# Decoder layer on one core: x rows in a home of their own, and the first attention's lead-in in a new order

## The reference

```python
u  = layernorm(x)
xn = layernorm(u) * gamma + beta
h  = dA * h + dB * xn[t]                       # a scan over the 1024 steps, 64 states per channel
y  = C . h + D * xn[t]
x1 = x + u + (y @ Wout.T + bout)
q  = layernorm(x1)                             # 16 heads of 16; keys and values are the context
x2 = x1 + softmax(q k.T / 4) v @ Wx.T + bx
z  = layernorm(x2)
g  = silu(z @ w1.T * s1) * (z @ w2.T * s2)     # 256 -> 1024, ternary weights with a scale per row
g  = gelu(g @ h1.T * t1);  g = gelu(g @ h2.T * t2)   # 1024 -> 1024, twice
out = x2 + g @ w3.T * s3
```

## Time and profile before

| what | us |
|---|---|
| median of 3 runs | 1010.57 |
| lowest, highest | 1008.23, 1010.67 |
| the profiled execution's own time | 1008.29 |
| its span, first to last instruction | 1006.6 |
| PE, DVE, ACT, POOL busy | 887.8, 527.2, 502.6, 188.1 |

### The profile page before, as it was taken

One profiled execution on the slowest core, in us unless ns is written; L12 is line 12 of the kernel. 1 busy time (PEld: TensorE's weight loads), 2 busy tenths in 40 slices (PEclk: granted clock), 3 DMA queues, 4 the chain that ended last, 5 costly groups with the idle time before them and its releaser, 6 DMA issues.

```text
span 1006.6 us, 15130 instructions
## 1 busy us (share of the span) xinstructions
PE 887.8 (88%) x5570; PEld 702.4 (70%) x5570; DVE 527.2 (52%) x877; ACT 502.6 (50%) x776; POOL 188.1 (19%) x207
## 2 busy tenths in 40 slices
PE   2038679669999999999999999999999999999996
PEld 0038567457787778777877777778777877777884
DVE  7975326455555555455545554556454645463411
ACT  2863514136644664466356635663566356635431
POOL 0864631022002200220022002200220021003000
PEclk9569889779999999999999999999999999999998
DMA  9976672510002000100010001000100020001000
GB/s 285 250 252 198 242 286 85 209 68 1 1 22 68 0 0 21 68 0 0 21 68 0 0 21 68 0 0 21 68 0 0 21 68 0 0 21 42 1 1 23
DMA packets 14632, 62.82 MB, mean 62 GB/s; under 512 B 2739, under 2 KB 4406, under 8 KB 13782
## 3 DMA queue, kind: packets, MB, share of 16 engines
q1 hardware_dynamic: 13862, 60.19, 17.5%
q10 hardware_dynamic: 704, 2.16, 0.7%
q0 software_dynamic: 32, 0.00, 0.0%
HBM read 50.16 MB, written 23.72 MB: 73 GB/s over the span
## 4 chain that ended last, share of the span: by engine, by line
PE 72%; DVE 12%; issue 7%; ACT 4%; DMA 4%; POOL 0%; SPq 0%; DVEq 0%; ACTq 0%; POOLq 0%
PE pair L1070 45%; PE pair L1057 10%; PE pair L1018 3%; DMA vblk<-in_ctx 3%; PE pair L1029 3%; PE pair L1045 2%; PE pair L462 2%; PE pair L995 2%; PE pair L1038 1%; DVE h1lo L889 1%; PE pair L469 1%; DVE tok L395 1%; DVE tok L391 1%; PE pair L527 1%; PE pair L476 1%
## 5 line engine op out<-in xcount | busy, mean ns | idle before, releaser
L1070 PE MATMUL pair<-h1hi,h_turned 128*128 128x512 f32 x512 | 204.7, 400 | 4.1 <-DVE h1lo L889 4.1
L770 ACT ACTIVATE vbuf<-pair,scl 128x512 f32<-128x512 f32 x128 | 87.6, 684 | 237.2 <-PE pair L1070 231.4
L1070 PE MATMUL pair<-h2hi,h_turned 128*128 128x512 f32 x512 | 202.6, 396 | 0.0
L1070 PE MATMUL pair<-h1lo,h_turned 128*128 128x512 f32 x512 | 199.8, 390 | 0.0
L1070 PE MATMUL pair<-h2lo,h_turned 128*128 128x512 f32 x512 | 199.6, 390 | 0.0
L889 DVE TENSOR_TENSOR h1lo<-vbuf,h1hi 128x512 fp32r<-128x512 f32 x80 | 61.8, 780 | 118.8 <-ACT h1hi L771 118.7
L1070 PEld LDWEIGHTS pair<-h1hi,h_turned 128*128 128x128 f32 x512 | 96.1, 188 | 39.7 <-issue 10.5
L1070 PEld LDWEIGHTS pair<-h2hi,h_turned 128*128 128x128 f32 x512 | 96.1, 188 | 25.2 <-issue 5.9
L1057 PE MATMUL pair<-zThi,w_turned 128*128 128x512 f32 x256 | 105.4, 412 | 5.2 <-DVE vbuf L918 2.6
L1070 PEld LDWEIGHTS pair<-h2lo,h_turned 128*128 128x128 f32 x512 | 96.2, 188 | 19.3
L1070 PEld LDWEIGHTS pair<-h1lo,h_turned 128*128 128x128 f32 x512 | 96.2, 188 | 18.6
(11 more groups left out here) (124 smaller groups left out, 1439.2 us busy)
## 6 DMA issues: line engine op xcount, KB each, us to landing
h_turned<-d_h SPq DMA_DIRECT2D x2, 4096.0 KB, 13.4
tok<-in_xs SPq DMA_DIRECT2D x8, 512.0 KB, 6.3
EE<-alpha_rows SPq DMA_DIRECT2D x16, 256.0 KB, 11.0
xres<-in_x SPq DMA_DIRECT2D x8, 512.0 KB, 4.0
x_rows<-x1t SPq DMA_DIRECT2D x8, 512.0 KB, 2.6
xr<-x_rows SPq DMA_DIRECT2D x8, 512.0 KB, 3.5
out<-xr SPq DMA_DIRECT2D x8, 512.0 KB, 2.7
x_rows<-xres SPq DMA_DIRECT2D x7, 512.0 KB, 2.7
```

The source lines that it names most:

```text
L770: e.activation(vb[:, s % 2, :], h_ps[s % 4], ACT.Gelu, scale=sc)
L1070: ins = e.matmul(bank, w[:, k, m * P:(m + 1) * P], src[part][:, k, :], start=(k == 0 and part == 0), stop=(k == HC - 1 and part == 1))
```

## The change

- `EE` moves to h1's later home and `xres` stays in h2's, so they no longer share. All rows of x are loaded right behind the first kernel matrices, without waits. h1 is loaded when the last `state` is done.
- SP's order: rings, x rows, attention's weights, keys and scales, context values and bias, then the copies and loads of w1, w2, w3 and the copy of h1, then the load of h1 and the copy of h2, then the x1 stores as before.
- POOL's mixer part is split: `natural_rows` ahead of the masks, head mask and the clearing of `vblk` ahead of its core stage, biases and masks 4 to 7 interleaved in a new way. ACT spreads `residual_base` over the octets and issues the later kernel matrices one octet sooner.
- Lead-in: four y buffers, y turned into two PSUM pairs, projected y into three, two probability buffers in the unused `GG`. `x1_add(0)`, the first attention projection, both layernorm turns and the z evacuation go by tiles or halves. Two of the y projections are moved behind the attention's end, and `x1_add(7)` behind `z_lo(0)`. In the blocks only the z evacuation, `z_lo` and the first gated product change.

```diff
-    EE = nc.alloc_sbuf_tensor_at("EE", [P, P, N], F32, offset=t["zone_b"])
+    EE = nc.alloc_sbuf_tensor_at("EE", [P, P, N], F32, offset=t["zone_e"])
     xres = nc.alloc_sbuf_tensor_at("xres", [P, TILES, DM], F32, offset=t["zone_b"])
+    def y_bank(i):
+        return pair[2 if i in (1, 3) else 0][:, :]
+    def p_bank(i):
+        return pair[3 if i == 0 else 2 if i in (5, 7) else 1]
...
         for g in range(4):
             tt_load(e, g)
+        for g in range(NBLK):
+            e.dma_start(xres[:, 4 * g:4 * g + 4, :], a["x"][:, 4 * g:4 * g + 4, :]).then_inc(xr_in[g], 16)
+        for n in ("xW", "keys", "scl"):
+            e.dma_start(t[n], a[n]).then_inc(k_in, 16)
+
+    def sync_weights(e):
         for n in ("w1", "w2", "w3", "h1"):
             e.dma_start(t["d" + n], a[n]).then_inc(w_d, 16)
...
+        e.wait_ge(w_d, 64)
+        for n in ("w1", "w2", "w3"):
             e.dma_start(t[n].bitcast(F32), t["d" + n]).then_inc(w_in, 16)
+        e.wait_ge(h_ps, NOCT)
+        e.dma_start(t["h1"].bitcast(F32), t["dh1"]).then_inc(w_in, 16)
+        e.dma_start(t["dh2"], a["h2"]).then_inc(h2_d, 16)
...
+    def gpsimd_core(e):
+        e.wait_ge(wo_in, 32)
+        done = 0
+        for g, until in ((4, 6), (5, 10), (6, 14), (7, 18), (None, TILES)):
+            for tile in range(done, until):
+                bias(e, tile)
+            done = until
+            if g is not None:
+                e.wait_ge(base_b, done)
+                mask(e, g)
+                e.wait_ge(t_mask, 2 * g + 2)
...
+            until = min(2 * o + 2 + max(0, o - 9), TILES)
+            for j in range(done, until):
+                residual_base(j)
...
-        e.wait_ge(m["h_scan"], NOCT)
         attn_loads(0)
         e.dma_start(xbo[:, :], a["xb"].partition_broadcast(P)).then_inc(S["xbo_in"], 16)
+        m["sync_weights"](e)
...
+        values_clear(0)
+        m["gpsimd_core"](e)
         e.wait_ge(m["h_scan"], NOCT)
         e.wait_ge(m["k_in"], 48)
         keys(0)
-        values_clear(0)
         rstd(0)
```

More of the change, by code:

```diff
@@ L209, in gpsimd @@
             inverse(b)
[L211 to L239, removed]
+        natural_rows(e)
+        e.wait_ge(natural, 5)
         for g in range(4):
-            mask(g)
+            mask(e, g)
         e.wait_ge(t_mask, 8)
[L243 to L249, removed]
+    def gpsimd_core(e):
[7 more added lines that the diff above has]
+                e.wait_ge(base_b, done)
+                mask(e, g)
+                e.wait_ge(t_mask, 2 * g + 2)
     def scalar(e):
@@ L437, in x1_add @@
         v = xres[:, 4 * i:4 * i + 4, :].rearrange("p j d -> p (j d)")
-        e.tensor_tensor(v if i > 0 else t["x1t"][:, :], pair[1][:, :], v, ALU.add).then_inc(x1a, 1)
+        e.tensor_tensor(v, p_bank(i)[:, :], v, ALU.add).then_inc(x1a, 1)
     def tensor(e):
@@ L749, in z_evac @@
             e.wait_ge(S["nat_t"], 2 * j + 2)
-            e.activation(zT[0][:, :], pair[3][:, :], ACT.Copy).then_inc(S["z_hi"], 1)
+            for k in range(DH):
+                e.activation(zT[0][:, k * BLK:(k + 1) * BLK], t_ps[k], ACT.Copy).then_inc(S["z_hi"], 1)
         def gated(i, attn):
@@ L882, in z_lo @@
         def z_lo(j):
-            e.wait_ge(S["z_hi"], j + 1)
-            e.tensor_tensor(zT[1][:, :], pair[3][:, :], zT[0][:, :], ALU.subtract).then_inc(S["z_lo"], 1)
+            for k in range(DH):
+                here = slice(k * BLK, (k + 1) * BLK)
+                e.wait_ge(S["z_hi"], DH * j + (k + 1))
+                e.tensor_tensor(zT[1][:, here], t_ps[k], zT[0][:, here], ALU.subtract).then_inc(S["z_lo"], 1)
         def low(i, n, dst):
@@ L996, in turn_nat, with lead_turn @@
             ins.then_inc(S["nat_t"], 1)
+        def lead_turn(n):
+            for k in range(TPB):
+                e.wait_ge(S["nat_rdy"], 4 * n + k + 1)
+                for h in range(DH):
+                    ins = e.transpose(pair[3][:, h * BLK + k * P:h * BLK + (k + 1) * P], nat[:, k, h * P:(h + 1) * P], ident[:, :])
+            ins.then_inc(S["nat_t"], 1)
         def turn_q(j):
-            e.wait_ge(S["z_lo"], j)
+            e.wait_ge(S["z_lo"], DH * j)
             turn_nat(2 * j)
@@ L1117, in _ @@
         y_turn, y_project = m["y_turn"], m["y_project"]
+        first, second = range(TPB // 2), range(TPB // 2, TPB)
+        e.wait_ge(m["k_in"], 48)
         y_turn(e, 0)
```

288 lines of the change are left out of this document (187 added, 101 removed).

## The result

| | us |
|---|---|
| before, median of 4 runs (range) | 1010.62 (1008.23 to 1011.21) |
| after, median of 4 runs (range) | 998.39 (995.75 to 1000.57) |
| ratio, 95% interval | 0.9892 [0.9872, 0.9912] |
| span of the profiled execution, before and after | 1006.6, 997.3 |

The kernel is 10.9 us faster by the ratio (8.9 to 12.9); between the two spans it is 9.3. The prediction said 1001, range 993 to 1008.

What follows compares the result with a forecast made beforehand. TensorE is busy nine tenths from the ninth slice on, so only the ragged first eight can gain. Third gated product 13.0 us earlier, less 2.0 restart and 2 core stage, is 9.0: 1001 us, range 993 to 1008.

Steps and rivals of the forecast that it cites:

- lost again at the restart: Behind the third gated product: PE restarts at the 1.2 GHz level after standing; bounds 1 and 2.7 us, taken 2.0.
- the queue behind h2: End of lead-in: x2 store and block 1's x1 load wait behind the h2 load; PE stands 21 us.
- Rival 4: End of lead-in: x1 rows of block 1 are not late, PE goes on at 182.5; about 978; chance 0.06.
- the lead-in's own length: First y transpose to last projection: 51.6 us of PE work plus 6.2 idle; sign: 55 to 62 us.
- Rival 6: Lead-in: TensorE's granted clock falls, at 0.75 costing 17 us more; time 1018; chance 0.07.
- the core stage: Mixer's core stage: 4.2 us more stops less gains 0.9 and 1.0, 2 later; bounds 5.5 earlier, 11.5 later.
- My other gain: End of core stage: last y evacuations no longer wait behind four residual rows; 0.9 us gained.
- my gain of 1.0: Before core stage: POOL's first masks no longer run beside DVE's gamma and beta passes; bounds 0 and 1.8 us earlier.
- the stops before 92 us: Core stage sign: two to four PE stops over 2.5 us, none after; wrong if summing under 4 or over 15.
- Rival 2: Core stage: PE's code waits for the whole 4 MB h1 copy; 17.2 us stops, 6.7 later, 1006; chance 0.13.
- Rival 3: Core stage: heavy traffic costs no more than quiet stops, 5 us in all; 5.5 earlier, 994; chance 0.08.
- the blocks: From block 1 on: nothing to gain; forecast wrong if blocks are not 100.2 us apart.

Runs made afterwards that it cites:

- Kernel 1: Changed kernel with SP's x2 store and block 1's x1 load issued before the 4 MB h2 load; 985.94 us, 0.9756 of before.
- kernel 2: Changed kernel with the x2 store and block 1's x1 load issued before both the h2 load and x1 store 7; 979.54 us, 0.9705 of before.
- 4: Changed kernel with each block's first gated product back in the old operand order with the old single wait; 996.37 us, 0.9862 of before.
- 7: Changed kernel with z evacuation and z_lo one instruction each again and the old first gated product; 995.73 us, 0.9866 of before.
- 12: Changed kernel with the wait for the last x1_add moved from the loop's scores to once ahead of the loop; 995.32 us, 0.9865 of before.
- Kernel 3: Changed kernel with the DRAM copies of w1, w2, w3, h1 and all behind them on SP held until the last state matmuls; 984.53 us, 0.9760 of before.
- kernel 9: Kernel before, with POOL's x1t + xbo rows held in the block loop until after DVE's two later h1lo instructions; 1002.20 us, 0.9938 of before.
- kernel 11: Changed kernel with weight copies held, x2 store and block 1's rows first, h2's copy after them, POOL's rows held behind h1lo; 963.02 us, 0.9556 of before.
- kernel 6: Changed kernel with weight copies held past the core stage, and x2 store and block 1's rows before x1 store 7 and h2 load; 972.63 us, 0.9631 of before.
- kernel 8: Changed kernel with only the 4 MB DRAM copy of h1 held until the core stage's last matrix is done; 988.27 us, 0.9796 of before.

## Why the prediction was right, and where not

| step | predicted | measured |
|---|---|---|
| first y transpose against before | 2 later | 7.65 later |
| from it to the end of the last projection | 57.8 | 55.9 (128.46 to 184.3) |
| end of x1_add(7) | 182.1 | 186.11 |
| from there to the third gated product | 23.3 | 23.9 |
| PE's gap | 21 | 21.5 |
| third gated product | 205.4 | 210.05 |
| lost again at the restart | 2.0 | 0.9 by the end of block 0 |
| blocks 1 to 6 | 0 | 3.7 gained |
| sum | 9.0 | 9.3 |

**Right: the queue behind h2.** The x2 store in h2's shadow (13.7 predicted, 14.0 found), x1_add(7) as the event that starts it, and the gap's size held to a microsecond. Kernel 1 shows that 11.6 of the 21.5 us are the queue behind h2, and kernel 2 that 5.2 more hang on x1_add(7) and its store. Rival 4 (not late) fell.

**Right: the lead-in's own length.** The window over it, after:

```profile
129.00:184.00 55.00, 51.15 (x299) 41.07 (x298) 36.35 (x61) 19.14 (x25) 6.25 (x9) 1.00 0.47 183
```

PE is busy 51.15 us there, and 52.0 from 128.46 to 184.3, where I had summed 51.6, at the full clock; what stayed idle is 3.9 us, not 6.2. POOL's power came at 136.80, where I said about 131; it stands 8.3 us behind the first y transpose, as foreseen, and that one was late. Rival 6 fell: no clock loss inside the lead-in.

**Wrong: the core stage, the term of the sum that was mis-sized.** I took 4.2 us of additional stops, and 2 later in all; measured were 7.65. The stops went from 8.6 to 15.7, 7.1 more. A second cost was not in my sum: PE needed 2.9 us more for the same matmuls (busy 48.6 for 45.7), at a mean clock of 0.82 where it had 0.94. I had charged that cost for the restart after the gap and forgotten it for the stops. Against both, the first state matmul came 2.45 us earlier in this execution (63.29, before 65.74), where I had taken 1.0. My other gain, 0.9 for the last y evacuations, was not there: from the start of the last 32 `carried` matmuls to the first y transpose it took 1.83 us before (118.98 to 120.81) and 1.93 after (126.53 to 128.46), so these evacuations had not waited for the residual rows. The profiled execution was also a late one: over the six kernels with the same core stage (after, 1, 2, 4, 7, 12) the first y transpose comes at 126.9 on average (124.3 to 128.5), over the three with the old one at 121.7 (120.8 to 122.2), so 5.2 later. The first state matmul itself came at 63.3 us in seven of the eleven executions with the new preparation and at 65.6 to 65.8 in four; the old ones had 65.7 to 65.9. What decides between the two is open, so my gain of 1.0 is neither shown nor refuted. Of my signs, the stops before 92 us sum to 10.2 for the three long ones, within 4 to 15, and two of them are over 2.5; but a third such stop, 3.38, came behind 92, where I had said none.

Rival 2 said almost the right sum, 17.2 us of stops and 6.7 later, by the wrong mechanism: no stop lasted as long as the 4 MB copy (11.4); the longest is 4.85, and three more lie between 2.1 and 3.4. Code passed while the copies ran: packets of it landed at 70.62 and 80.10 us, and the load of w1, which waits for the last copy, was issued at 81.19. In 70.7 to 79.1 us the copies held the engines with packets of 58 KB, 2.9 us each. Rival 3 (traffic costs nothing) fell: without it the stops are 2.6. The Trainium skill, "Runtime: NRT & Kernel Launch", section "Instruction fetch mechanics", calls the refill of code mostly hidden. Kernel 3 agrees, with 2.6 us over a stage of 48; the changed kernel does not, with 15.7.

**Missed: the blocks.** I wrote that they would stay 100.2 us apart and that the forecast was wrong otherwise. That sign failed. It is luck that its 3.7 us came in where the core stage took 5.65 us too much: with 1.9 from a lead-in that was shorter than forecast and 1.1 from the restart they made up for that and for 0.9 lost on the way to the third product, and the sum came out at 9.3 for 9.0. I had also written that the blocks leave nothing to gain; kernel 9 takes 0.9 us off each. The Trainium skill, "SBUF — State Buffer", section "Who interferes with whom", says that a VectorE instruction with two inputs in SBUF contends with a GpSimd instruction that reads SBUF, and that one with at most one input in SBUF, outside the 2-port modes, does not. The rows agree: a h1lo, with both inputs in SBUF, took up to 1.22 us beside GpSimd's rows and 0.69 without them, and the gate multiply, which reads one of its two tensors from PSUM, kept its 0.75 beside the same rows.

## What to carry to other kernels

When a lead-in is shortened, ask first what the next thing is that stands in a queue for no reason of data: by their ratios, the whole change gained 11 us, one moved line in the old kernel 6.8, and three added waits and four moved calls in the new one another 34 (kernel 11 against the changed kernel). Background transfers are not free to an engine that runs fast through straight-line code. Put the bulk of them where it goes through its code slowly: kernel 3's lead-in, straight-line too, needs 640 matmuls and weight loads in 60 us where its core stage needs 3073 in 48, and beside 358 GB/s no stop of PE without a releaser is listed there. And count the clock after each long stop as well as the stop. And when held transfers move, look at who is queued behind them at the new place (kernel 6) before adding the two gains up.

## What the runs showed of the hardware

- PE's stops without a releaser are waits for its code: in fourteen traces each of the 65 over 0.45 us ended 1.0 to 1.7 us after a 16 KB packet of the instruction queue had landed. In the quiet stage of kernel 3 the first two packets started 0.3 us after PE had entered the block before, in the changed kernel's the first five 4.9 to 10.7 us after it.
- The sum of these stops in a core stage of 1536 matmuls: 2.6 us with none of the 5 us windows from 65 to 105 us above 200 GB/s (kernel 3), 6.6 and 8.6 with two (kernel 8 and the kernel before), 15.7 with five (the changed kernel). Over the six kernels with the changed kernel's core stage it varies between 11.4 and 15.7.
- After four stops of 2.1 to 4.9 us in the changed kernel the granted clock stood at 0.50 for 3.4 to 6.8 us; beside stops of up to 1.3 us in kernel 3 it stayed at 1.00. The same 1536 matmuls kept PE busy for 48.6 and 44.7 us.
- A 512 KB store right behind a 4 MB load took 14.0 to 14.4 us to land, ahead of it 2.6; behind the held weights and h2's copy, 19.9 (median of seven).
- Two DVE instructions with both inputs in SBUF took 2.36 or 1.83 us for the pair, by how GpSimd's four tensor_tensor met them, and 1.48 with those held behind; the gate multiply, with one of its two tensors in PSUM, kept its 0.75 in all.
